# Reordering the slots of the first attention, and its front, in a fused two-layer attention kernel

## What is computed

```
x = x + xattn0(norm(x), ctx)   # 16 heads of 64, rope on q and k, mask per sequence and key
x = x + ffn0(norm(x))          # int4-quantised 128x128 weight, bias, rank-16 addition
x = x + xattn1(norm(x), ctx)   # 16 heads of 8, biases, one mask
x = x + ffn1(norm(x))          # quantised gated block, 512 wide
```

## Time and profile before

| | |
|---|---|
| median of 3 runs | 728.89 us (728.0 to 730.18) |
| the profiled execution | 727.17 us, of which 725.3 are its span |
| TensorE products, loads | busy 681.5 us (94%), 570.5 us (79%) |
| VectorE, GpSimd, ScalarE | busy 531.1 (73%), 433.1 (60%), 387.0 us (53%) |
| chain that ended last | PE 75%, DVE 13%, POOL 5%, issue 3%, ACT 3%, DMA 1% |
| slot 0 to slot 29 | 35.1 to 430.3 us |

### The profile page before, as it was taken

One profiled execution on the slowest core, in us unless ns is written; L12 is line 12 of the kernel. 1 busy time (PEld: TensorE's weight loads), 2 busy tenths in 40 slices (PEclk: granted clock), 3 DMA queues, 4 the chain that ended last, 5 costly groups with the idle time before them and its releaser, 6 DMA issues.

```text
span 725.3 us, 23490 instructions
## 1 busy us (share of the span) xinstructions
PE 681.5 (94%) x9246; PEld 570.5 (79%) x9251; DVE 531.1 (73%) x1649; ACT 387.0 (53%) x846; POOL 433.1 (60%) x560
## 2 busy tenths in 40 slices
PE   8699999999999999999999989999999999998775
PEld 6488788888888888888889868788888888875444
DVE  5666676767667678567677645777888878877996
ACT  2325345444453533544435453566666766766896
POOL 3567856766586586496488333456565555632675
PEclk9889999999999999999999999999999999999999
DMA  9401012011011101101101020000000000000011
GB/s 266 125 11 58 2 38 61 7 36 45 17 45 45 35 3 45 36 26 36 36 6 31 31 78 7 7 11 7 11 6 4 9 4 4 4 1 2 24 44 51
DMA packets 26767, 23.82 MB, mean 33 GB/s; under 512 B 7149, under 2 KB 23357, under 8 KB 26681
## 3 DMA queue, kind: packets, MB, share of 16 engines
q1 hardware_dynamic: 25864, 22.25, 10.9%
q10 hardware_dynamic: 816, 0.36, 0.2%
HBM read 10.25 MB, written 2.10 MB: 17 GB/s over the span
## 4 chain that ended last, share of the span: by engine, by line
PE 75%; DVE 13%; POOL 5%; issue 3%; ACT 3%; DMA 1%; SPq 0%; ACTq 0%; DVEq 0%
PE bank L1261 7%; PE bank L1219 7%; PE bank L1241 7%; PE bank L1883 6%; PE bank L1117 5%; PE bank L1223 4%; PE bank L1916 4%; PE bank L1118 4%; PE bank L1119 4%; PE bank L1252 3%; PE bank L1901 2%; DVE a_am L873 2%; DVE f_h_max L2133 2%; PE bank L1168 2%; PE bank L1857 1%
## 5 line engine op out<-in xcount | busy, mean ns | idle before, releaser
L722 POOL TENSOR_TENSOR a_turned<-a_turned,a_rope 128x512 f32<-128x512 f32 x63 | 81.8, 1298 | 50.1 <-DVE a_turned L826 50.1
L723 POOL TENSOR_TENSOR a_qr<-a_straight,a_turned 128x512 f32<-128x512 f32 x64 | 81.5, 1273 | 4.9
L1002 ACT CAST a_qb<-a_qr 128x512 bf16<-128x512 f32 x64 | 40.0, 624 | 69.2 <-POOL a_qr L723 69.2
L823 DVE TENSOR_TENSOR a_straight<-bank,a_rope 128x512 f32<-128x512 f32 x63 | 43.2, 685 | 34.5 <-PE bank L1119 33.4
L1219 PE MATMUL bank<-a_qr,a_kr 64*77 64x128 f32 x960 | 62.2, 278 | 5.1 <-DVE a_wk_lo L918 2.6
L1241 PE MATMUL bank<-a_vs,a_probs 77*64 77x65 f32 x2048 | 66.8, 223 | 0.0
L1241 PEld LDWEIGHTS bank<-a_vs,a_probs 77*64 77x64 f32 x2048 | 62.4, 137 | 4.5 <-issue 1.3
L734 POOL TENSOR_TENSOR a_k_turned<-a_k_turned,a_rope 128x308 f32<-128x308 f32 x61 | 47.9, 786 | 25.9 <-DVE a_k_turned L836 25.9
L1261 PE MATMUL bank<-a_wo,a_oTn 128*128 128x128 f32 x512 | 62.7, 276 | 0.6 <-ACT a_oTn L1027 0.6
L1219 PEld LDWEIGHTS bank<-a_qr,a_kr 64*77 64x77 f32 x960 | 54.3, 148 | 10.2 <-issue 7.4
L1261 PEld LDWEIGHTS bank<-a_wo,a_oTn 128*128 128x128 f32 x512 | 60.4, 192 | 1.5 <-ACT a_oTn L1027 0.8
(11 more groups left out here) (274 smaller groups left out, 1945.1 us busy)
## 6 DMA issues: line engine op xcount, KB each, us to landing
a_vs<-a_stage SPq DMA_DIRECT2D x16, 312.8 KB
out<-x_all SPq DMA_DIRECT2D x16, 128.0 KB, 1.8
x_all<-in_x_dram SPq DMA_DIRECT2D x7, 256.0 KB, 5.8
a_vs<-a_stage SPq DMA_DIRECT2D x4, 308.8 KB
a_mask_in<-in_mask SPq DMA_DIRECT2D x16, 77.0 KB, 5.6
a_wv<-in_ctx SPq DMA_DIRECT2D x16, 77.0 KB
a_ctx_in<-in_ctx SPq DMA_DIRECT2D x8, 128.0 KB
a_vs<-a_stage SPq DMA_DIRECT2D x4, 211.2 KB
```

The costliest lines, as they stand in the source:

```text
L722: steps.link(nc.gpsimd.tensor_tensor(tv, tv, rope[:, 1:2, :].broadcast_to([128, 4, S]), ALU.mult))
L723: nc.gpsimd.tensor_tensor(qr[P][:, 2 * k:2 * k + 2, :, :].rearrange("p t j s -> p (t j) s"), sv, tv, ALU.subtract if made else ALU.add).th ...
```

## The change

1. Key groups per quad go from 2, 4, 1, 1 to 2, 4, 2, 0 (first quad: slots 0 to 3 from 4, 4, 2, 2 to 4, 6, 2, 0).
2. Even slots: the first key group goes ahead of the queries, the last ones between the maxima and the fourth query group, none at the tail (slot 0: one, two, and one).
3. Odd slots: next rows ahead of the output projection, maxima ahead of the values, turned maxima right behind the values, turned rows of b's output last. VectorE normalises the next rows first, and takes the maxima ahead of `normalise`. Where there are no key groups, the first value half stands in their place.
4. Front: key groups 2 and 3 are finished by VectorE (`whole_keys`), which writes `kr` itself, and GpSimd does groups 0 and 1 only. The count of GpSimd's groups is corrected by `keys_roped`. The key weights are split ahead of the first key cast and ahead of the first maxima. 26 instead of 10 idle products ahead of the first maxima, and six more ahead of their turn.
5. Loads: query weights first, then mask 0, first part of context 0, rope table; the second part of context 0 and mask 1 ahead of context 1.

```diff
-    KEYS, LATE_KEYS = {0: range(4, 8), 1: range(8, 11), 2: range(12, 14), 3: range(14, 16)}, {1: range(11, 12)}
+    KEYS, LATE_KEYS = {0: range(4, 8), 1: range(8, 12), 2: range(14, 16)}, {1: range(12, 14)}
...
-        KEYS[4 * q + 2], KEYS[4 * q + 3] = range(n + 6, n + 7), range(n + 7, n + 8)
+        KEYS[4 * q + 2] = range(n + 6, n + 8)
...
+    def first_keys_in(b):
+        return KEYS.get(b, ())[:1]
+    def middle_keys(b):
+        return KEYS[0][1:3] if b == 0 else ()
+    def last_keys(b):
+        return KEYS.get(b, ())[3 if b == 0 else 1:]
+    def odd_keys(b):
+        return KEYS.get(b, ())[:2], KEYS.get(b, ())[2:]
...
-    MADE = (1, 2, 3)
+    MADE, WHOLE = (1,), (2, 3)
+    def keys_roped(n):
+        return n if n <= 2 else max(2, n - 2)
...
-        load_context(0)
+        sp.dma_start(wq[:], t["Wq0"]).then_inc(first_weights_in, 16)
         load_mask(0)
-        for dst, src in ((wq[:], t["Wq0"]), (rope[:], t["c_rope"])):
-            sp.dma_start(dst, src).then_inc(first_weights_in, 16)
+        load_context(0, (0,))
+        sp.dma_start(rope[:], t["c_rope"]).then_inc(first_weights_in, 16)
...
+        load_mask(1)
+        load_context(0, (1,))
         load_context(1)
-        load_mask(1)
...
+        def whole_keys(n):
...
+            steps.did(nc.vector.tensor_tensor(flat4(spare), flat4(bank[:, 0:QK]), rope[:, 3:4, 0:KL].broadcast_to(shape), ALU.mult))
+            steps.link(nc.vector.tensor_tensor(flat4(bank[:, 0:QK]), flat4(bank[:, 0:QK]), rope[:, 2:3, 0:KL].broadcast_to(shape),
+                                               ALU.mult))
+            steps.link(nc.vector.stream_shuffle(turned_keys, spare, mask=[lane ^ 1 for lane in range(32)]))
+            nc.vector.tensor_tensor(out, view(bank[:, 0:QK]), view(turned_keys), ALU.subtract).then_inc(
+                a_free[TASK[name][0]], 1)
...
-        for n in range(4):
-            (first_keys if n in MADE else rope_keys)(n)
+        rope_keys(0)
+        first_keys(1)
+        whole_keys(2)
+        whole_keys(3)
         masks(1, 1)
         normalised_rows(1)
+        dve.wait_ge(keys_split, 1)
+        nc.vector.tensor_tensor(wk_lo[:], wk[:], wk_hi[:].bitcast(F32), ALU.subtract).then_inc(keys_split, 1)
         maxima(0, 0, 0)
         split_turned(("C",))
         split_turned(("X", 1))
-        dve.wait_ge(keys_split, 1)
-        nc.vector.tensor_tensor(wk_lo[:], wk[:], wk_hi[:].bitcast(F32), ALU.subtract).then_inc(keys_split, 1)
...
             else:
+                ahead, behind = odd_keys(b)
...
-                for n in keys_in(b)[:2]:
-                    rope_keys(n)
                 if more_pre(p):
                     masks(p + 2, P)
+                    normalised_rows(p + 2)
+                for n in ahead:
+                    rope_keys(n)
                 residual(b - 1)
-                for n in keys_in(b)[2:]:
+                if more_pre(p) and ahead:
+                    split_turned(("X", p + 2))
+                for n in behind:
                     rope_keys(n)
...
+                if more:
+                    maxima(b + 1, 1 - P, 0)
+                if more_pre(p) and not ahead:
+                    split_turned(("X", p + 2))
                 normalise(b)
                 if pair(p, PAIRS - 2):
                     t["start"].statistics(steps, 0)
-                if more:
-                    maxima(b + 1, 1 - P, 0)
...
-                if more_pre(p):
-                    normalised_rows(p + 2)
                 for n in late_keys(b):
                     rope_keys(n)
-                if more_pre(p):
-                    split_turned(("X", p + 2))
...
-            act.wait_ge(k_roped, keys_of(b))
+            act.wait_ge(k_roped, keys_roped(keys_of(b)))
+            if b < 4:
+                for n in WHOLE:
+                    read(act, ("K", n))
...
+        nc.scalar.copy(wk_hi[:], wk[:]).then_inc(keys_split, 1)
         cast_keys(0)
...
-                exps(b, (0, 1) if last_pair(p) else (3, 0, 1))
+                exps(b, (0, 1) if last_pair(p) else (3, 0))
                 turned_out(b - 1, 0)
                 turned_out(b - 1, 1)
-                exps(b, (2, 3) if last_pair(p) else (2,))
+                exps(b, (2, 3) if last_pair(p) else (1, 2))
+                if more_pre(p) and ahead:
+                    transposed(("X", p + 2))
                 if more:
                     cast_queries(p + 1, 1 - P, 3)
                     cast_keys(b + 1)
...
-        idle_products(10)
+        idle_products(26)
         score_maxima(0, 0, 0)
         transposes(("C",))
         transposes(("X", 1))
+        idle_products(6)
         turn_maxima(0, 0, 0)
-        pe.wait_ge(keys_split, 2)
...
             elif j == 0:
                 all_scores(b, P, j)
+                if first:
+                    pe.wait_ge(keys_split, 2)
+                for n in first_keys_in(b):
+                    project_keys(n)
                 project_queries(p + 1, (0, 1))
...
                 score_maxima(b + 1, P, 1)
+                for n in last_keys(b):
+                    project_keys(n)
                 project_queries(p + 1, (3,))
...
-                for n in keys_in(b):
-                    project_keys(n)
...
                 all_scores(b, P, j)
                 turn_out(b - 1)
-                for n in keys_in(b)[:2]:
+                for n in ahead:
                     project_keys(n)
-                if few:
+                if u is not None and not ahead:
                     project_values(u, 0)
+                if more_pre(p):
+                    transposes(("X", p + 2))
                 out_projection(b - 1)
-                for n in keys_in(b)[2:]:
+                for n in behind:
                     project_keys(n)
+                score_maxima(b + 1, 1 - P, 0)
                 for r in range(3):
                     values(b, P, j, r)
-                if u is not None and not few:
-                    project_values(u, 0)
-                score_maxima(b + 1, 1 - P, 0)
+                turn_maxima(b + 1, 1 - P, 0)
                 if u is not None:
+                    if ahead:
+                        project_values(u, 0)
                     project_values(u, 1)
-                turn_out(b)
-                turn_maxima(b + 1, 1 - P, 0)
                 for n in late_keys(b):
                     project_keys(n)
-                if more_pre(p):
-                    transposes(("X", p + 2))
+                turn_out(b)
```

More of the change, by code:

```diff
@@ L518, in pa_tasks @@
             if b % 2 == 0:
-                yield from queries[:2] + tasks(front_keys(b)) + queries[2:] + values + tasks(keys_in(b))
+                yield from (tasks(first_keys_in(b)) + queries[:2] + tasks(middle_keys(b)) + queries[2:3] + tasks(last_keys(b))
+                            + queries[3:] + values)
+                continue
+            ahead, behind = odd_keys(b)
+            rows = [("X", p + 2)] if p + 2 < PAIRS else []
+            if ahead:
+                yield from tasks(ahead) + rows + tasks(behind) + values + tasks(late_keys(b))
             else:
-                yield from tasks(keys_in(b)) + values + tasks(late_keys(b)) + ([("X", p + 2)] if p + 2 < PAIRS else [])
+                yield from values[:1] + rows + values[1:]
     TASK, count = {}, [0, 0]
@@ L756, in slot @@
                     rope_turn(p + 1, 1 - P, 2)
+                for n in last_keys(b):
+                    rope_keys(n)
+                if more:
                     rope_turn(p + 1, 1 - P, 3)
-            for n in keys_in(b):
-                rope_keys(n)
-            for n in late_keys(b):
-                rope_keys(n)
+            else:
+                ahead, behind = odd_keys(b)
+                for n in (*ahead, *behind, *late_keys(b)):
+                    rope_keys(n)
             if j == 1 and pair(p, PAIRS - 2):
@@ L1084, in slot @@
                     cast_keys(b + 1)
-                if u is not None:
+                if u is not None and not ahead:
                     values_in(u, 0)
-                    values_in(u, 1)
+                if more_pre(p) and not ahead:
+                    transposed(("X", p + 2))
                 if more:
                     fold_in(b + 1)
-                if more_pre(p):
-                    transposed(("X", p + 2))
+                if u is not None:
+                    if ahead:
+                        values_in(u, 0)
+                    values_in(u, 1)
                 if last_pair(p):
```

63 lines of the change are left out of this document (40 added, 23 removed).

## The result

The changed kernel takes 737.16 us (median of 4 runs, 736.74 to 740.1) against 728.89: a ratio of 1.0121 with a 95% interval of 1.009 to 1.0151. The forecast was 724.9, the sign is wrong.

A forecast was written before the change was run, and what follows sets the result against it. TensorE, at work nearly all the time, was taken as the bound, with its winnable gaps and a clock fall in the front. -3.9 - 2.4 + 0.2 + 2.7 - 0.6 = -4.0 us gave 724.9 against the median 728.89; range 717 to 730.

The forecast's parts named there:

- slot 0 at 31.2: Front: slot 0 begins at 31.2 us instead of 35.09, -3.9 us.
- slot 0 takes 15.4: Slot 0: 15.4 us instead of 17.81 with the clock at the 2.4 GHz level, -2.4 us.
- The loads: Front: reordered loads taken as 0, bounds 0.5 us won or 1.9 us lost if the mask comes later.
- -6.1 for the front and slots 1 to 3: Start to slot 4: front -3.9, slot 0 -2.4, slots 1 to 3 +0.2 us.
- The repeated part: Quads after slot 3: three of each sort, 3 x 0.7 + 3 x 0.2 = +2.7 us.
- The pair 4q+2, 4q+3: Second kind of even and odd slot: 25.1 us against 24.65, even slot 12.1, two new waits of 0.75.
- the pair 4q, 4q+1: First kind: even slot gains 0.2 us; odd slot -0.25 where no values stand in 4q, +0.2 in quads with values.
- Slot 29: Wins 1.7 us by losing the late maxima, but meets the cast (1.1): -0.6 us.
- Rival 1: Repeated part wins too, as if all added waits were hidden: 715.3 us; chance 0.17.
- Rival 2: Clock falls all the same, at gaps around 27 us or in slot 0, losing 2.7 us: 727.6; chance 0.11.
- Rival 3: Cast for the maxima bounds every odd slot, 0.5 us later in all 14, 7 us on top: 731.9; chance 0.13.
- Rival 4: Front gives less, the mask or second value half binding, 1.6 to 2.5 us: 727; chance 0.1.

The follow-up runs named there:

- the run with the rows on ScalarE: Whole change, but from the third pair on ScalarE makes the normalised rows from VectorE's scale and shift: 727.58 us, 0.9983 of the kernel before.
- the run with a PSUM operand: Whole change, but VectorE's row normalisation reads its scale as a second tensor from a PSUM bank: 726.13 us, 0.9982 of the kernel before.
- the rows last: Whole change, but normalised rows made behind the maxima again and turned at the odd slot's end: 724.68 us, 0.9948 of the kernel before.
- GpSimd's work thinned: Changed kernel, but GpSimd leaves out the queries' sine products from the second pair on (wrong results): 722.59 us, 0.9912 of the kernel before.
- front only: Kernel before with the new loads, first key groups, key weights and idle products, slots unchanged: 722.3 us, 0.9909.
- slot 29: Kernel before with the new front, rows ahead on ScalarE, and slot 29 alone in the change's order: 716.46 us, 0.9812.
- the two last runs: Front, ScalarE's rows and slot 29 reordered, timed side by side: mask behind the query weights 716.2 us (0.983), mask ahead 714.92 us (0.9817).
- the run with the rows in the middle: Kernel before with only VectorE's row normalisation moved ahead, right behind the masks: 729.27 us, 1.0008.

## Why the prediction was wrong

**Where the 8.8 us come from.** Ratios of the runs, each times 728.9, in the order in which parts are added; each step is uncertain by about 2 us, so only the first and the last are clear of noise by much.

| added | ratio | step |
|---|---|---|
| the front | 0.9909 | -6.6 |
| keys 2, 4, 2, 0 and the new even slots | 0.9943 | +2.5 |
| maxima ahead of the values, turned rows last | 0.9948 | +0.4 |
| next rows ahead, without the contention | 0.9983 | +2.6 |
| their normalisation on VectorE beside GpSimd | 1.0121 | +10.1 |

The fourth row is the run with the rows on ScalarE; the run with a PSUM operand gives the same ratio, 0.9982. The traces support less of it: from slot 4 to slot 28 they have 315.70 us with the rows last, 315.77 with a PSUM operand and 318.05 with the rows on ScalarE. What the rows' place costs without the contention is thus between nothing and 2.6 us.

**The step that failed** is the move of the normalised rows in the odd slots. The prediction gave it no price: it took the next rows' turn to hang on its bank alone ("so it waits for the 0.7 us to VectorE and its 0.9 of reading: 0.7 idle") and so left the two row instructions at the 344 ns that they have behind the maxima. Moved ahead of the residual they meet GpSimd at its queries, take 1391 ns in the median, and hold up both the turn and the key reading behind them. It also says of GpSimd that it "works through two key groups and four queries without a pause", and draws from it what comes late on ScalarE, not what that does to VectorE. The 344 ns were the duration at the old place, and the prediction carried them to the new one. The trace of before had two signs of it, the minimum, median and maximum of the mask's instruction (L776: 244, 340, 856 ns) and one of them in slot 11, beside a GpSimd product that began at 189.69. Timeline of the kernel before:

```profile
189.69 0.84 POOL L736 TENSOR_TENSOR a_kr<-a_k_straight,a_k_turned 128x308 f32<-128x308 f32 x1
189.90 0.72 DVE L776 TENSOR_SCALAR a_am<-a_mask_in 128x154 bf16<-128x154 int32 x1
```

0.72 us for an instruction of 0.24 in the earlier trace rows, ending at 190.62, just behind GpSimd's at 190.53: what lies so beside GpSimd has a longer form, and a move to such a place has to be priced by it.

The Trainium skill states the rule, and the prediction should have weighed it. "SBUF — State Buffer", SBUF: two separate sides, calls the port pair that VectorE and GpSimd share an exclusive lock: the one that starts first has it for its whole instruction, the other is blocked; ScalarE never waits there. The Trainium skill, "VectorE: DVE Perf Modes", Mode 2×_2P — use both read ports for one tensor, has a single SBUF source, f32 included, read through both ports, of which one is shared. The rows here agree: 1391 ns in the median beside products of 1.3 us, 344 with GpSimd's work thinned, 344 beside a full GpSimd once an operand is in PSUM, and 478 to 498 ns for each of the 28 on ScalarE.

**The front, point by point.** Predicted: slot 0 at 31.2, measured 32.08 in the profiled execution of the change, but 31.07, 31.27 and 31.32 in three other kernels with the same front (front only, rows on ScalarE, slot 29). Most of the difference is the clock's: after an idle of 2.77 us the profiled execution was granted 0.57 from 10.5 to 13.5, and from its first projection at 12.30 it took 19.78 us to slot 0, where the front only took 19.12 from 11.95. The steps between came as predicted in the front only: key cast at 27.01 (26.9), first maxima at 28.02 (28.1), VectorE's maxima at 29.19 (29.4). Predicted: slot 0 takes 15.4 and stays at the 2.4 GHz level; measured 15.19 at 1.00, and 15.36 with the front only, where slot 0 keeps its old order. So the gain is the clock's alone. That the sum met it is partly luck: it leaves out the 1.23 us that slot 0 had idle before and yet takes 0.5 of them off, and by its own terms comes to 13.9 + 0.7 + 2.0 = 16.6; the new gaps were smaller than priced, since slot 0 of the change is idle for 1.02 in all. Predicted: slot 4 at 88.1; 87.62 with the front only, 87.70 and 88.28 with the whole change and the rows by PSUM or on ScalarE, 90.03 in the change. The loads, taken as 0 between -0.5 and +1.9, came out so: the rope table's cast begins 1.1 earlier (7.66), the mask 1.0 later (6.38), and the two last runs put the mask's part at 1.0. The Trainium skill, "DMA: Bandwidth & Descriptors", Queues, rings and completion order, which the prediction cited, has each DMA engine consume its descriptors in ring order. The prediction's landing of the mask by that order was 6.1, and the traces agree: VectorE took it up at 6.38 and 5.93 behind the weights, at 4.40 ahead of them. So -6.1 for the front and slots 1 to 3 was right within 0.4 us.

**The repeated part** was forecast at +2.7 over six quads, 104.6 for the first two. Without the contention the two take 105.36 with a PSUM operand, 106.13 with the rows on ScalarE. The 0.77 between these is the ScalarE run's own: its two row instructions stand ahead of its casts, TensorE waits 3.6 us in 8 for the key cast instead of 1.0 in 2, and its slots 4q+3 take 12.8 instead of 12.5. The forecast was thus 0.8 too low for two quads; from slot 4 to slot 28 the PSUM run takes 4.9 us more than the kernel before (315.77 against 310.84, slot 4's first score product standing at 94.02), where 2.7 were forecast. The pair 4q+2, 4q+3 came out right in sum, 24.96 against 25.1, but split otherwise: 12.50 instead of 12.1 for the even slot, 12.46 instead of 13.0 for the odd one. What was mis-sized is the pair 4q, 4q+1: slots 4 and 5 take 0.5 more than before instead of 0.2, slots 8 and 9 take 0.2 more instead of 0.25 less. Of the waits, the key reading is 0.28 instead of 0.15 and the bank of the next rows' turn 0.67 as forecast (0.7); the turned rows are 0.30 instead of 0.75, and the cast at the maxima, forecast at 0.75 in each slot 4q+3, shows only from slot 27 on. In the changed kernel the two quads take 110.81, of which 1.5 in the profiled execution is again the clock.

**Slot 29** was forecast at -0.6: it is -1.2 with the change (11.76 against 12.96) and -1.3 with slot 29 reordered alone (11.62). The wait for the cast there is 0.5 instead of 1.1.

**The rivals.** Rival 1 (the repeated part wins too) fell: even without contention it loses. Rival 2 (the clock falls all the same) did not happen in the gap meant, but fell at two others. Rival 3 named the slower side, though little over a third of the size (3.0 us over the kernel before where 8.3 were measured; by its words a quad over 53.5, and the quads took 54.6 and 56.2), and its mechanism is not what was seen: TensorE waited 0.5 us for a key cast once in the first attention of the changed kernel, and for VectorE's rows and readings 17.5. Rival 4 was worth 1.0 at the most. The chance of 0.13 for slower covered only waits for GpSimd's and ScalarE's results; no case let an instruction's own duration change with its place.

## What to carry to other kernels

Before an instruction of VectorE from SBUF to SBUF is moved, look at what GpSimd does at the new place, and price it as ending no earlier than GpSimd's running instruction; the spread of its durations in the old trace (min, median, max) tells whether it has ever met one. Where it has to stand there, a second operand in PSUM, or ScalarE, takes it out of GpSimd's way: each was worth 10 us here. And a change of several parts is best run with each part's addition: this one held a front worth 6.6 us and a slot 29 worth 1.2 us inside a loss.

## What the runs showed of the hardware

**The wait goes in either direction.** In the trace of before a subtraction of VectorE with two SBUF inputs runs into GpSimd's products:

```profile
15.66 1.28 POOL L723 TENSOR_TENSOR a_qr<-a_straight,a_turned 128x512 f32<-128x512 f32 x1
...
16.58 1.44 DVE L908 TENSOR_TENSOR a_wv_lo<-a_wv,a_wv_hi 128x1024 fp32r<-128x1024 f32 x1
16.90 2.29 POOL L722 TENSOR_TENSOR a_turned<-a_turned,a_rope 128x512 f32<-128x512 f32 x1
```

It starts while one of them runs (to 16.94) and is 0.2 us longer than its like in the earlier trace rows (1.23); GpSimd's next product then takes 2.29 instead of 1.29 and ends 1.17 after VectorE's end at 18.02. The start stamps don't tell who has precedence: in slot 9 VectorE's normalisation is stamped 0.02 us ahead of GpSimd's product and waits all the same. GpSimd's instruction before that (159.43, 0.84) ran to 160.27, so neither began beside an idle neighbour, and these stamps can neither show nor refute that the first to start has it.

**The drawn-out instruction ends 0.1 us behind GpSimd's.** The ends are 162.94 and 162.85 in slot 9, 169.98 and 169.90 in the run with the rows in the middle, 190.62 and 190.53 for the mask's instruction in the trace of before. Alone they take 0.34 and 0.24 us, so by these stamps they don't stand still for the whole of GpSimd's instruction and run after it; which part of them waits is not shown. The block cited above is thus borne out for their ends, not for their whole length.

**The wait is invisible in a view of idle times.** The row instructions count as busy while they wait, so VectorE looks 75% busy instead of 73%, and the wait for it stands in TensorE's list only. The mean duration of a group, set against before, is the view that shows it.

**The clock can fall after shorter idles than the one of 3.73 us in the earlier trace rows.** In the profiled execution of the change it fell after 2.77 us idle in the front and after 2.01 in slot 9, where 16 products of the output projection then took 3.47 us instead of the 1.95 of the earlier trace rows. After 1.27 us, at 136.80, it did not, nor after 2.02 us at 274.71 and 2.00 at 383.90 in the same execution, where the 16 products took 1.95. In the other executions of the same kernel the mean clock was 0.998 to 1.000 against 0.991 in this one, so the same idles do not always bring it down; what decides is not shown.
